# Masking transposed scores after the exponential on GpSimd, with the value and sum products adjacent

## The reference, cut to what matters

```python
scores = jnp.einsum('bhir,bhjr->bhij', q_lr, k_lr) * scale
causal_mask = jnp.triu(jnp.ones((Tq, Tq), dtype=bool), k=1)
scores = jnp.where(causal_mask, jnp.float32(-jnp.inf), scores)
attn = jax.nn.softmax(scores, axis=-1)
y = jnp.einsum('bhij,bhjd->bhid', attn, v)
...
x = _layernorm(x + y @ Wo.T + bo)
```

## Time and profile before

| | us |
|---|---|
| median of 3 runs | 4449.62 |
| lowest, highest | 4447.46, 4454.19 |
| profiled execution, its own time | 4442.53 |
| its span | 4440.4 |
| TensorE matmul busy | 3988.6 |
| VectorE busy | 2297.3 |
| ScalarE busy | 1434.1 |
| GpSimd busy | 469.8 |

### The profile page before, as it was taken

One profiled execution on the slowest core, in us unless ns is written; L12 is line 12 of the kernel. 1 busy time (PEld: TensorE's weight loads), 2 busy tenths in 40 slices (PEclk: granted clock), 3 DMA queues, 4 the chain that ended last, 5 costly groups with the idle time before them and its releaser, 6 DMA issues. The chain is left out here.

```text
span 4440.4 us, 61118 instructions
## 1 busy us (share of the span) xinstructions
PE 3988.6 (90%) x22121; PEld 2616.8 (59%) x22121; DVE 2297.3 (52%) x3990; ACT 1434.1 (32%) x2018; POOL 469.8 (11%) x349
## 2 busy tenths in 40 slices
PE   5999999999999999999999771689999999999990
PEld 3655555545545555555455331568888888888880
DVE  4365554554564545545545466645444544454444
ACT  0332332332323323323323340133333333333324
POOL 2011011010020110100100100001111111011100
PEclk6999999999999999999999895589999999999995
DMA  4222332232322223321323270044433443344328
GB/s 146 53 82 77 77 91 70 53 89 82 96 64 75 75 77 77 91 82 45 85 81 72 86 253 10 5 138 126 128 116 116 124 130 116 116 122 132 117 67 312
DMA packets 192890, 439.27 MB, mean 99 GB/s; under 512 B 38144, under 2 KB 40192, under 8 KB 183936
## 3 DMA queue, kind: packets, MB, share of 16 engines
q1 hardware_dynamic: 172944, 384.22, 28.6%
q0 software_dynamic: 14336, 34.09, 4.1%
q10 hardware_dynamic: 5376, 17.83, 1.0%
HBM read 261.95 MB, written 72.38 MB: 75 GB/s over the span
## 5 line engine op out<-in xcount | busy, mean ns | idle before, releaser
L718 DVE TENSOR_REDUCE max_slots<-shared_banks 128x1 f32<-128x512 f32 (+3 forms) x1536 | 805.5, 550 | 627.0 <-PE shared_banks L528 530.8
L663 ACT ACTIVATE probs<-scores_t 128x1024 f32<-128x1024 f32 (+3 forms) x768 | 612.7, 811 | 903.4 <-PE scores_t L562 532.2
L1561 PE MATMUL m_ps_h<-m_tokens_t,m_w_parts 128*128 128x512 f32 x3072 | 740.6, 391 | 1.6 <-DVE m_tokens_t L1499 1.6
L1561 PE MATMUL m_ps_y<-m_w_parts,m_hidden_parts 128*128 128x512 f32 x3072 | 737.1, 390 | 0.5
L525 PE MATMUL shared_banks<-k_operands,q_operands 96*128 96x512 f32 (+3 forms) x1536 | 618.0, 430 | 65.0 <-DVE max_slots L718 52.9
L1561 PEld LDWEIGHTS m_ps_y<-m_w_parts,m_hidden_parts 128*128 128x128 f32 x3072 | 575.5, 188 | 125.3 <-issue 6.2
L1561 PEld LDWEIGHTS m_ps_h<-m_tokens_t,m_w_parts 128*128 128x128 f32 x3072 | 576.0, 188 | 120.4 <-issue 2.0
L525 PEld LDWEIGHTS shared_banks<-k_operands,q_operands 96*128 96x128 f32 x1536 | 294.3, 195 | 522.9 <-DVE max_slots L718 347.7
L559 PE MATMUL scores_t<-q_operands,k_operands 128*128 128x512 f32 (+3 forms) x1536 | 505.3, 401 | 20.8 <-ACT probs L663 13.9
L1468 ACT ACTIVATE m_hidden<-m_ps_h,m_b 128x512 f32<-128x512 f32 x256 | 176.6, 690 | 818.7 <-PE m_ps_h L1561 805.6
L1526 DVE CAST m_hidden_parts<-m_hidden 128x512 fp32r<-128x512 f32 x256 | 111.2, 434 | 584.9 <-ACT m_hidden L1468 584.9
(11 more groups left out here) (209 smaller groups left out, 3349.6 us busy)
## 6 DMA issues: line engine op xcount, KB each, us to landing
m_w_raw<-in_w1T SPq DMA_DIRECT2D x64, 1024.0 KB, 5.1
m_w_raw<-in_w2T SPq DMA_DIRECT2D x64, 1024.0 KB, 8.7
q_operands<-natural SPq DMA_DIRECT2D x384, 128.0 KB, 2.4
k_operands<-natural SPq DMA_DIRECT2D x384, 128.0 KB, 2.5
wqk_group<-scratch_wqk SPq DMA_DIRECT2D x32, 1024.0 KB, 5.2
natural<-in_xT SPq DMA_DIRECT2D x8, 2048.0 KB, 7.6
x_residual<-in_x SPq DMA_DIRECT2D x64, 256.0 KB, 2.6
scratch_x<-x_tile SPq DMA_DIRECT2D x64, 256.0 KB, 2.0
```

The lines of the kernel that those rows point to most:

```text
L663: act.activation(probs[:, slot_of(k, pair), :, c0:HALF], st[:, pair, :, c0:HALF], ACT.Exp, scale=SCALE).then_inc(exp_done, 1)
L718: dve.tensor_reduce(mx[:, h, slot:slot + 1], src[:, 0:n], AX.X, ALU.max).then_inc(bank_free[bank], 1)
L1561: mm = pe.matmul(bank, a, b, start=(first and n == 0), stop=(final and n == len(pairs) - 1))
```

## The change

Six things change together. (1) The mask matmul L562 and its constant are gone; instead GpSimd runs one affine_select per diagonal step and head pair on the first 128 columns of `probs`, with zeros above the diagonal, and values of a diagonal step wait for it. (2) No max item is dealt behind a values item any more; its share goes behind the sums. So values and sums of one step stand next to each other. (3) split_x is cut into 8 pieces, two at each values item of steps 4 to 7 of group 2. (4) normalise is called at the item at which VectorE has inverted the last piece; before, it was called at the end of the half, and for the last half of a batch after the bias addition of out 2. (5) VectorE's rule for the pieces moves to `pieces_at`, shared with GpSimd, and is the same rule. (6) One memset and one select less in the set-up.

```diff
 plan_step:
-        if first <= n < final:
+        if first <= n < final and part[0] != "values":
             share = m * (n + 1 - first) // (final - first)
...
+        def pieces_at(item, left):
+            if ends_half(item):
+                return left
+            if left == 0 or not uses_bank(item):
+                return 0
+            if item[0] == "out":
+                return left if item[1] in (0, 2) else 1
+            return 1 if item[0] != "max" or item[2] % 2 == 0 else 0
+        SPLIT_FROM = DC
...
 GpSimd:
+            def mask_probs(b, g, k, pair):
+                c0 = steps[k][2]
+                s = (b * GROUPS + g) * NE + k
+                block = probs[:, slot_of(k, pair), :, c0:c0 + P]
+                plain(pool, exp_done, 2 * s + pair + 3, pool_passed)
+                pool.affine_select(out=block, in_=block, compare_op=ALU.is_ge, fill=0.0, base=0,
+                                   pattern=[[0, 2], [1, P]], channel_multiplier=-1).then_inc(masked, 1)
...
                 for item in order:
-                    if ends_half(item) and item[1:] != (GROUPS - 1, NE - 1):
-                        normalise(b, item[1], steps[item[2]][0])
-                    if item == ("proj", GROUPS - 2, 3) and not (isinstance(b, int) and b == NB - 1):
-                        split_x(b + 1)
+                    left -= pieces_at(item, left)
+                    if half is not None and left == 0:
+                        normalise(b, *half)
+                        half = None
+                    if ends_half(item):
+                        half, left = (item[1], steps[item[2]][0]), DEN_PIECES - 1
+                    if item[0] == "scores" and diagonal[item[2]]:
+                        mask_probs(b, *item[1:])
+                    if more and item[0] == "values" and item[1] == GROUPS - 2 and 0 <= item[2] - SPLIT_FROM < DC:
+                        for piece in range(2):
+                            split_x(b + 1, 2 * (item[2] - SPLIT_FROM) + piece)
                     if item[0] != "out":
                         continue
                     t = item[1]
                     pool.wait_ge(res_in[t % 2], 16 * (b * (TT // 2) + t // 2 + 1))
                     pool.tensor_tensor(xres[:, t % 2], xres[:, t % 2], keep["bo"][:], ALU.add).then_inc(bo_added, 1)
-                    if t == 2:
-                        normalise(b, GROUPS - 1, 1)
...
 TensorE, scores:
-                    mm = pe.matmul(out[:, c0:HALF], k_ops[...], q_ops[...], start=True, stop=not diag)
-                    if diag:
-                        mm = pe.matmul(out[:, c0:c0 + P], identb[:], mask_k[:], start=False, stop=True)
+                    mm = pe.matmul(st[:, pair, q, c0:HALF], k_ops[...], q_ops[...], start=True, stop=True)
 TensorE, values:
-                pe.wait_ge(exp_done, 2 * s + 4)
+                if diagonal[k]:
+                    pe.wait_ge(masked, (b * GROUPS + g) * N_DIAG + masked_through(k))
+                else:
+                    pe.wait_ge(exp_done, 2 * s + 4)
```

More of the change, by code:

```diff
@@ L267, in build_attention @@
         mask_q = sb("mask_q_rows", [P, P], BF16)
-        mask_k = sb("mask_k_rows", [P, P], BF16)
         shared = ps("shared_banks", [P, 2, HALF])
@@ L282, in build_attention @@
         st_full, exp_done, pv_done, normed = sem("st_full"), sem("exp_done"), sem("pv_done"), sem("normed")
+        masked = sem("masked")
         y_drained, den_drained, rden_ready = sem("y_drained"), sem("den_drained"), sem("rden_ready")
@@ L288, in build_attention @@
             sem("rstd_ready"), sem("x1_ready"))
-        N_CONSTS = 6
+        N_CONSTS = 5
         STRIPS = 16 * 2 * len(Q_STRIPS)
@@ L306, in build_attention, with masked_through @@
         assert PROB_BUFS == 4 and (2 * NE) % PROB_BUFS == 0
+        diagonal = [j * P >= hh * HALF for hh, j, _ in steps]
+        N_DIAG = 2 * sum(diagonal)
+        def masked_through(k):
+            return 2 * sum(diagonal[:k + 1])
         def ends_half(item):
             return item[0] == "sums" and steps[item[2]][1] == 4 * steps[item[2]][0] + 3
+        def pieces_at(item, left):
[7 more added lines that the diff above has]
+        SPLIT_FROM = DC
         def turns(order, base):
@@ L408, in _ @@
             pool.memset(mask_q[:], 0.0).then_inc(own_zeros, 1)
-            pool.memset(mask_k[:], 0.0).then_inc(own_zeros, 1)
-            pool.wait_ge(own_zeros, 3)
+            pool.wait_ge(own_zeros, 2)
             pool.affine_select(out=ident[:], in_=ident[:], compare_op=ALU.not_equal, fill=1.0, base=0,
@@ L418, in _, with split_x @@
                                pattern=[[-1, P]], channel_multiplier=1).then_inc(consts, 1)
[L419 to L426, removed]
+            def split_x(n, piece):
+                c = piece % DC
+                if piece == 0:
+                    await_parts(pool, pool_passed, n - 1, GROUPS - 2)
+                    plain(pool, x_in, 16 * (n + 1), pool_passed)
+                if piece < DC:
                     ins = pool.tensor_copy(xs[:, HI, c, :], nat[:, c, :])
-                ins.then_inc(x_split, 1)
-                pool.wait_ge(x_split, 2 * n + 1)
-                for c in range(DC):
+                else:
+                    if piece == DC:
+                        pool.wait_ge(x_split, 2 * n + 1)
                     ins = pool.tensor_tensor(xs[:, LO, c, :], nat[:, c, :], raw(xs[:, HI, c, :]), ALU.subtract)
-                ins.then_inc(x_split, 1)
+                if c == DC - 1:
+                    ins.then_inc(x_split, 1)
+            def mask_probs(b, g, k, pair):
[5 more added lines that the diff above has]
+                                   pattern=[[0, 2], [1, P]], channel_multiplier=-1).then_inc(masked, 1)
             def normalise(b, g, hh):
@@ L443, in run @@
                 order, _, _ = scope(b)
+                more = not (isinstance(b, int) and b == NB - 1)
+                left, half = 0, None
                 for item in order:
-                    if ends_half(item) and item[1:] != (GROUPS - 1, NE - 1):
-                        normalise(b, item[1], steps[item[2]][0])
-                    if item == ("proj", GROUPS - 2, 3) and not (isinstance(b, int) and b == NB - 1):
-                        split_x(b + 1)
+                    left -= pieces_at(item, left)
[9 more added lines that the diff above has]
+                            split_x(b + 1, 2 * (item[2] - SPLIT_FROM) + piece)
                     if item[0] != "out":
@@ L556, in scores @@
                     h = 2 * pair + q
[L557 to L560, removed]
-                    if diag:
-                        mm = pe.matmul(out[:, c0:c0 + P], identb[:], mask_k[:], start=False, stop=True)
+                    mm = pe.matmul(st[:, pair, q, c0:HALF], k_ops[:, buf, h, j * P:(j + 1) * P],
+                                   q_ops[:, buf, h, hh * HALF + c0:(hh + 1) * HALF], start=True, stop=True)
                 mm.then_inc(st_full, 1)
@@ L683, in run @@
                     kind = item[0]
+                    for _ in range(pieces_at(item, len(pieces))):
+                        invert(b, *pieces.pop(0))
                     if ends_half(item):
-                        while pieces:
-                            invert(b, *pieces.pop(0))
                         n = 2 * (b * GROUPS + item[1]) + steps[item[2]][0]
@@ L697, in run @@
                     src = shared[:, bank, :]
[L698 to L702, removed]
                     if kind == "proj":
```

## The result

The change makes the kernel slower: 4499.13 us (median of 4 runs) against 4451.24, a ratio of 1.0104 with a 95% interval of 1.0088 to 1.0120. The prediction was 4508 in a range of 4454 to 4550, with 0.81 on slower.

What follows compares the result with a forecast made beforehand. TensorE was taken to set the pace. On the profiled 4442.5 us: groups +5, last group -2, late bias addition +21, low clock +25 and +10, sum +59, so 4501.5 profiled, 4508 median; range 4454 to 4550.

Steps and rivals of the forecast that it cites:

- Mask matmuls: Diagonal steps on TensorE: removing them saves 0.16 us a pair, together 2.0 us a group.
- Selects hidden: GpSimd selects at diagonal steps and group openings: 0.45 us each, hidden, at the opening just so; no cost.
- the pieces of x: Split_x subtractions on GpSimd, two of 2.4 us between the selects of steps 8 and 9: cost nothing.
- which VectorE instructions could contend with GpSimd: Shared SBUF interfaces: reductions read PSUM, so only layer norm additions could suffer, and no select runs beside them.
- Bursts and the drain: Max items in attention groups: new stalls where three follow each other 3.3 us, longer wait after half 0 0.9.
- adjacency: Values next to sums at 8 sites a group: 0.25 us saved each, 2.0 us a group.
- The forecast net of a group: One attention group: -2.0 - 2.0 + 3.3 + 0.9 = +0.2 us, +5 over 31 groups.
- Bias addition behind normalise: Out 2 on GpSimd: layer norm 2 starts later, delaying out 4 by 2.6 us a batch, +21.
- The clock: Low TensorE clock following longer waits: +25 after half 0, +10 at out 4.
- Rival A: Attention and out 4: the clock doesn't follow the longer waits, only +24, 4474; chance 0.2.
- rival B: Group opening: the select is on the path, 4518 at 0.8 us, 4540 with semaphore round trips; chance 0.09.
- rival C: Slots S2 to S9 and after half 0: bursts hardly cost, no new stalls, 4353; chance 0.12.

Runs made afterwards that it cites:

- Changed kernel with filler: Changed kernel plus unread matmuls in TensorE's two long waits, after half 0 and before out 4: 4446.41 us, ratio 0.9996.
- kernel before with filler: Kernel before plus 3 unread matmuls of 512 columns in TensorE's wait after half 0: 4429.81 us, ratio 0.9954.
- experiment 5: Changed kernel with max items dealt as before the change, so values and sums stand apart again: 4441.99 us, ratio 0.9981.
- experiment 6: Changed kernel without selects, the mask back as a matmul on TensorE: 4538.48 us, ratio 1.0205.
- drain_free_mask: drain_free without selects, the mask back as a matmul on TensorE: 4410.18 us, ratio 0.9905.
- drain_free: Changed kernel, out 2's bias before normalise, max items dealt evenly, none behind half 0's last sums or next scores, later denominator pieces moved: 4382.48 us, ratio 0.9850.
- Experiments 1 and 2: Changed kernel with out 2's bias added before normalise: 4467.84 us, ratio 1.0040; kernel before with normalise ahead of that bias: 4485.03 us, ratio 1.0078.
- experiment 7: Changed kernel with every select done twice, one after the other: 4518.78 us, ratio 1.0155.
- drain_apart: drain_free with max items dealt behind values too, so values and sums stand apart: 4403.53 us, ratio 0.9896.

## Why the prediction was right, point by point

The two fillers split the result into waits and clock. Changed kernel with filler less kernel before with filler is 0.9996 - 0.9954 = 0.42 points, 19 us: what the change costs at a steady clock. The clock costs the changed kernel 48 us and the kernel before 20, so 28 come from there. That the two make up the measured 46 (0.0104 x 4451) but for rounding is no check: it follows from how they are taken. What the runs test is each part against its forecast, 24 and 35.

- **Mask matmuls, -2.0 us a group: right.** 2.0 by experiment 5. It is the price in that order only: 1.4 by experiment 6 and 0.8 by drain_free_mask. Its parts were off against each other: two pairs of 256 take 840.58 - 839.92 = 0.66 us where the same stretch before had 1.12 (953.76 in rows 3 to 954.88), 0.23 a pair and not 0.16.
- **Selects hidden: right, and just so.** 0.41 us each (0.45 taken, bounds 0.28 and 0.8); values(0) starts 0.05 us behind the select. At most 0.27 us of it shows at an opening, 9 us in 32 groups. That the pieces of x cost nothing held for the changed kernel and not for drain_free (1.3 us in that group). The prediction's sentence on which VectorE instructions could contend with GpSimd read its own rows wrongly: the layer norm's additions read one operand from shared_banks, that is PSUM. No contention shows anyway: VectorE is busy for 36.47 and 36.36 us in groups with 9.07 and 22.31 us of GpSimd work, 36.64 before.
- **Bursts and the drain, +4.2, against adjacency, -2.0: right in kind, over-sized in sum.** The forecast net of a group, with the masks, was +0.2 us; measured is 62.16 - 62.58 = -0.42. Each distance came out within some 0.1 us (1.29 for 1.28, 2.69 for 2.8). What I mis-sized is both sums, each a little: TensorE's idle in the group grew by 3.8 us (62.16 - 55.89 against 62.58 - 60.09) and not 4.2, its busy time fell by 4.2 and not 4.0.
- **Bias addition behind normalise, +21: right.** 3.05 us idle for some 3, where it was 0.21: 2.84 a batch, 23. Experiments 1 and 2 give 28 and 35 with its low clocks.
- **The clock, +35 net: right in kind.** Net +28. That the waits alone bring the clock down was argued then, and is shown now by both fillers, which end the low clock by filling the waits. The number of stretches was right (33 of them with 150 us up to 2450 us, by the trace's clock record, against 11 with 38; 23 more were forecast), the price was not: in the kernel before, 20 us for 38 us of low clock taken away by the filler, in the changed kernel 48 for 140 (10 us stayed low). TensorE is busy in 144 of the changed kernel's 150 us at the low clock, so it doesn't stand idle in them; that slower matmuls use up idle time which the changed group has more of would explain the lower price, and is not shown. By place the forecast was close as well: 26 of the 33 stand behind half 0 (27 groups were forecast), and a low clock follows the wait at out 4 in all 8 batches (6 were forecast).

Rival A (no clock, 4474) is refuted by the filler, rival B (select on the path) by the rows and by experiment 7, rival C (bursts cost nothing) by the rows: 0.65 us of idle ahead of the third max of a burst, 2.19 after half 0, and 3.8 us more idle in a group. What the bursts cost apart from the wait after half 0 no run shows.

The forecast was 59 and 46 came. The clock term was 7 too high. At a steady clock the forecast was 5 - 2 + 21 = 24 and 19 were measured. That is in part luck: a group in the middle of a batch is not 0.2 us longer but shorter. Measured from one end of half 0 to the next in the two traces with filler, the 24 such intervals inside a batch are 8.6 us shorter together in the changed kernel (0.36 each), and the 7 with a batch's outputs are 26.3 us longer, 3.8 each, of which the wait at out 4 is 2.9. A few low clocks are left in the first trace and counted in. Together that is 17.7. So around the outputs a group is some 0.9 us longer, where the others are shorter; why is open.

## What to carry to other kernels

When two buffers are taken strictly in turn, count how many items stand in one slot: the third waits for the first one's round trip (1.29 us here, of which 0.65 were idle), though the second engine is busy for only 36 of 62 us. An edit that takes 4 us of work from the bounding engine is worth nothing if a sibling edit builds waits of that size. And whenever a call is moved in an in-order queue (here normalise past one bias addition), read who waits for what now stands behind it.

## What the runs showed of the hardware that I had not expected

Useless matmuls in a wait made the kernel before 0.46% faster and the changed one 1.08% faster: a wait of 0.97 us, with two of 0.2 behind it, was followed in a third of the groups by TensorE's clock granted at 1.2 instead of 2.4 GHz for 3.4 us.

The wait alone doesn't decide it: drain_apart waits 1.19 us behind half 0 in each group, and its clock is low for 10 us up to 2450, while drain_free waits 0.33 us there and has 41 us, and 9 of its 11 stretches stand 32 to 34 us behind that point. A kernel with less TensorE work may lose part of its gain to the clock: behind the same 0.97 us wait experiment 5 has 65 us of low clock and the kernel before 34, in one execution of each.

In the stretch of the changed kernel at 0.50 TensorE was busy for 6.25 of 6.80 us: busy share alone would not have told that anything was wrong there.
